# One strided four-column addition written as four one-column additions, in front of each scan of a recurrent layer

## The reference, cut to what matters

```python
dt = softplus(einsum('blhr,dr->blhd', dt_x, dt_proj_w) + dt_proj_b)
A = -exp(A_log)
def step(h, inp):
    dt_t, b_t, c_t, u_t = inp
    a_bar = exp(dt_t[..., None] * A[None, :, None, :])
    h = a_bar * h + (dt_t * u_t)[..., None] * b_t[:, :, None, :]
    y_t = einsum('bhds,bhs->bhd', h, c_t)
    return (h, y_t)
```

## Time and profile before

| | us |
|---|---|
| median of 3 runs | 17432.16 |
| the profiled execution | 17420.92 |
| its span (first to last instruction, slowest core) | 17419.6 |
| VectorE busy | 9252.5 (53%) |
| GpSimd busy | 6204.1 (36%) |
| TensorE matmuls busy | 5463.1 (31%) |
| ScalarE busy | 3186.6 (18%) |

### The profile page before, as it was taken

One profiled execution on the slowest core, in us unless ns is written; L12 is line 12 of the kernel. 1 busy time (PEld: TensorE's weight loads), 2 busy tenths in 40 slices (PEclk: granted clock), 3 DMA queues, 4 the chain that ended last, 5 costly groups with the idle time before them and its releaser, 6 DMA issues.

```text
span 17419.6 us, 75091 instructions; the slowest of 8 cores (17391.7 to 17419.6 us)
## 1 busy us (share of the span) xinstructions
PE 5463.1 (31%) x11019; PEld 1117.8 (6%) x11019; DVE 9252.5 (53%) x6045; ACT 3186.6 (18%) x3440; POOL 6204.1 (36%) x2692
## 2 busy tenths in 40 slices
PE   1123322222222222466553422222222222237555
PEld 0001000000000000011110100000000000001111
DVE  0023388888888888200003348888888888720011
ACT  0022322221222121100002331222122221101000
POOL 0000066666666666000000026666666666500000
DMA  2211100000000000210111110000000000020111
GB/s 54 64 41 35 49 4 4 4 4 4 4 4 4 4 4 3 62 35 23 42 44 41 36 44 4 4 4 4 4 3 4 4 4 4 15 72 16 31 41 41
DMA packets 760229, 378.17 MB, mean 22 GB/s; under 512 B 545528, under 2 KB 689112, under 8 KB 758752
## 3 DMA queue, kind: packets, MB, share of 16 engines
q1 hardware_dynamic: 759776, 373.37, 8.1%
HBM read 222.62 MB, written 148.91 MB: 21 GB/s over the span
## 4 chain that ended last, share of the span: by engine, by line
DVE 29%; DMA 21%; issue 16%; PE 16%; POOL 13%; ACT 3%; SPq 2%; DVEq 1%; POOLq 0%; ACTq 0%
DVE pf L269 19%; PE ps_mm L280 14%; POOL pb L234 13%; DVE pb L230 4%; DVE s_tmp L230 3%; ACT pf L275 2%; DMA s_rd<-g_dt 2%; DMA pb<-g_mid 2%; SPq L217 2%; PE ps_t L286 1%; DMA g_xsc<-colA 1%; DMA g_ct<-s_bc 1%; DMA g_bt<-s_bc 1%; DMA pf<-g_xn 1%; DVE pf L230 1%
## 5 line engine op out<-in xcount | busy, mean ns | idle before, releaser
L234 POOL TENSOR_TENSOR pb<-pb 128x2048 bf16<-128x2048 bf16 x768 | 3271.7, 4260 | 7720.2 <-ACT pb L275 5526.5
L269 DVE TENSOR_TENSOR_SCAN pf<-pf,pb 128x2048 f32<-128x2048 f32 x768 | 4090.4, 5326 | 607.5 <-DMA g_y<-s_yev 217.6
L234 POOL TENSOR_TENSOR pb<-pf,pb 128x512 bf16<-128x512 f32 x1920 | 2932.3, 1527 | 1243.9 <-DVE pf L269 951.1
L230 DVE TENSOR_TENSOR pb<-pf,pb 128x512 bf16<-128x512 f32 x1152 | 3024.5, 2652 | 141.5 <-DVE pf L269 135.2
L280 PE MATMUL ps_mm<-pb 128*128 128x512 bf16 x4608 | 2616.3, 589 | 1157.2 <-DMA pb<-g_y 288.2
L280 PE MATMUL ps_y<-pb,s_yd 128*16 128x512 bf16 x1536 | 799.8, 590 | 5145.3 <-DVE pb L230 4514.9
L275 ACT ACTIVATE pf<-ps_mm,s_acol 128x2048 f32<-128x2048 f32 x768 | 1441.5, 1977 | 2657.3 <-PE ps_mm L280 2657.3
L230 DVE TENSOR_TENSOR pf<-pf 128x512 f32<-128x512 f32 (+1 forms) x288 | 216.4, 751 | 1964.2 <-ACT pf L275 1045.2
L280 PE MATMUL ps_mm<-s_rd,s_pd 64*128 64x512 bf16 (+1 forms) x1024 | 596.4, 582 | 1723.7 <-ACT pf L275 1480.0
L225 DVE CAST pb<-pf 128x512 bf16<-128x512 f32 (+3 forms) x427 | 206.3, 494 | 1737.4 <-DMA pf<-g_xsc 599.1
L280 PE MATMUL ps_r<-pb,s_yd 128*16 128x512 bf16 x1536 | 830.9, 593 | 949.9 <-POOL pb L234 949.7
(11 more groups left out here) (70 smaller groups left out, 2544.0 us busy)
## 6 DMA issues: line engine op xcount, KB each, us to landing
pf<-x SPq DMA_DIRECT2D x64, 512.0 KB
g_xn<-pf SPq DMA_DIRECT2D x64, 256.0 KB
g_dt<-pb SPq DMA_DIRECT2D x256, 64.0 KB
s_rd<-g_dt SPq DMA_DIRECT2D x256, 64.0 KB
pf<-g_xn SPq DMA_DIRECT2D x64, 256.0 KB
g_x<-pf SPq DMA_DIRECT2D x64, 256.0 KB
g_mid<-pb SPq DMA_DIRECT2D x128, 128.0 KB
pb<-g_mid SPq DMA_DIRECT2D x128, 128.0 KB
```

Source lines behind the costliest of these rows:

```text
L230: o.tensor_tensor(out=d, in0=x, in1=y, op=op), waits)
L234: o.tensor_tensor(out=d, in0=x, in1=y, op=op), waits)
L269: return S.op("v", lambda o, d=dst, a0=d0, a1=d1: o.tensor_tensor_scan(out=d, data0=a0, data1=a1, initial=0.0, op0=ALU.mult, op1=ALU.add), ...
```

## The change

The addition of `s_tmp` to `w` at the 4 first positions is no longer one instruction on a pattern of 4 elements but a loop of 4 instructions, each on 1 element per partition. The first waits for `s_tmp` and for `w`; each later one waits for the one before it, and the memset for the last. What is computed is the same.

```diff
                 else:
                     m_t1 = vtt(s_tmp.ap(), a_seg, cs, ALU.mult,
                                waits=[m_exps[k][ti], m_carry[ti]])
-                    m_t2 = vtt(w_seg, w_seg, s_tmp.ap(), ALU.add,
-                               waits=[m_t1, m_w])
+                    m_t2 = m_t1
+                    for d in range(DH_SUB):
+                        wcol = AP(pb, w_i * 1024 + d * TC,
+                                  [[PB_N * 1024, 128], [1, 1]])
+                        m_t2 = vtt(wcol, wcol,
+                                   s_tmp.ap()[:, d:d + 1], ALU.add,
+                                   waits=[m_t2, m_w if d == 0 else None])
                     m_fx = vmemset(a_seg, 0.0, waits=[m_t2])
```

## The result

| | before | four columns |
|---|---|---|
| median of 8 runs, us | 17430.78 | 17930.91 |
| lowest to highest | 17416.53 to 17528.88 | 17923.64 to 17938.97 |
| ratio to before, 95% interval | | 1.0282 [1.0265, 1.0299] |
| span of the profiled execution | 17419.6 | 17929.1 |
| chunk with a carry, from scan to scan | 77.08 | 82.47 |

The change costs 500 us, 2.8%.

The account below looks back on a forecast made before the run. The prediction took one chain alternating between VectorE and GpSimd as the bound. Per chunk 1.18 + 3 x 0.95 + 2 x 1.32 = 6.67 us, over 96 chunks 640, gave 18,065 us, range 17,950 to 18,150.

Parts of the forecast that it names:

- One chain from scan to scan: Recurrences: work passes between VectorE and GpSimd, so instructions between `s_tmp` and scan lie on the path; 6.67 us per chunk.
- the rival that has GpSimd set the pace: Chunk head: columns fill VectorE's 7 to 8 us of idle time, giving 17,421 to 17,440 us; chance 0.02.
- The price of a step: Each extra column on VectorE: 0.315 us, 0.177 for the instruction and 0.14 for the wait behind it.
- the free tiles: Tiles 1, 3 and 5: GpSimd has finished its products, so three extra steps run unhindered, costing 0.95 us each tile.
- Columns 1 and 2 of tiles 2 and 4 held up: Tiles 2 and 4: the first two columns wait for GpSimd's products, costing 1.32 us per tile.
- The sum: Chunks with a carry: 6.67 us each over 96 chunks, 640 us in all.
- the won race: Rival, tiles 2 and 4: column 2 precedes GpSimd's third product, 1.01 us instead of 1.32; 18,002 us; chance 0.06.
- Tile 0: the second column waits for GpSimd's second `w`: Tile 0: column 1 gets in first, column 2 is held until that `w` ends, near 3.8 us; cost 1.18.
- Waits aren't free: Between dependent columns: 0.14 us per wait, against the skill's no-cost rule, with a step near 0.11, some 190 us.
- The errata figure: One-column addition: the skill's 58 cycles plus elements gives 61 ns, three free steps 0.61 us; set against 0.177 measured.
- The range: Whole kernel's time: from 17,950 us, past the rival with column 2 ahead, up to 18,150.

Follow-up runs that it names:

- vprod: The kernel before with all four products with C on VectorE, `w` still on GpSimd: 16817.46 us, ratio 0.9635.
- vall: The kernel before with `w` and all products with C on VectorE, GpSimd idle in the recurrence: 14554.02 us, ratio 0.8336.
- ms3: The kernel before with three chained memsets of a 128x4 scratch tile between its addition and its memset: 17671.14 us, ratio 1.0119.
- rep4: The kernel before with three more 128x4 additions (of zeros) behind its own, each waiting for the last: 17987.79 us, ratio 1.0299.
- late2: The four-column kernel with one more wait instruction, for something long done, ahead of column 2: 18033.01 us, ratio 1.0334 to the kernel before.
- late4: The four-column kernel with one more wait instruction, for something long done, ahead of column 4: 18027.90 us, ratio 1.0325 to the kernel before.
- nowait: The four-column kernel with no waits among the columns, only the first one waiting: 17642.31 us, ratio 1.0081 to the kernel before.

## Why the prediction was right or wrong, point by point

- **One chain from scan to scan, nothing of GpSimd left over to cover an extra instruction.** Right for tiles 1, 3 and 5, too strong for the others. VectorE's idle time at a chunk's head stayed at 711 us and the chunks without a carry at 70.1 us (70.0 with the change); nothing of the cost was hidden there, and the rival that has GpSimd set the pace, with a cost near nothing, is dead. vprod and vall show from the other side that the two engines take turns. But in tile 0 the scan waited 3.4 us for GpSimd and in tiles 2 and 4 0.6 us, and that time can be filled: ms3's three memsets cost 0.06 us or less there. The sum didn't suffer by it, since a column, other than a memset, waits for GpSimd itself. I had also misread the products: in tiles 0 to 3 they follow `w` after 0.20 us; GpSimd is idle only ahead of those of tiles 4 and 5.
- **The price of a step, 0.315 us. This is the step that failed.** The mechanism was right, an instruction and the wait behind it, one after the other; the size was not. A step is 0.267: 0.163 for the instruction and 0.104 for the wait. I had read the wait off the distance from the addition to the memset, 0.14, but what follows a column is another addition. The earlier trace rows had the right number: `s_tmp` ends at 4046.45 and the addition starts 0.17 later behind *two* waits. A second wait instruction adds 0.07 (the distance between the two in the trace), which leaves 0.10 for one, and in vall, where only one wait stands between them, 0.10 is what the rows show. rep4 confirms it for additions of 4 elements (0.28 apart), ms3 gives the memset's 0.20 (0.06 and 0.14). Three steps, and 0.01 off the last, shorter addition, make 0.79 for the 0.95 that I had; the free tiles paid 0.83, 0.77 and 0.74, tile 0 1.08 instead of 1.18.
- **Columns 1 and 2 of tiles 2 and 4 held up, 1.32 us.** Wrong, and mostly by the same error. The memset at 4058.83 came 0.03 behind GpSimd's product. An addition starts 0.04 sooner than a memset would, and the first column ends 0.01 sooner than the addition of 4 elements did, so column 2 comes 0.02 ahead. I gave this rival 0.06 and weighed it with the memset's start. These tiles paid 0.97 and 1.00. late2 against late4 shows the race itself; losing it costs a whole step more, 0.27 x 192 = 51 us.
- **The sum.** 96 x 5.39 = 517 us in the recurrences, against 640. The lost 123 us are some 50 of the race and some 70 of the step. Putting one of them right would not have been enough: the won race alone gives 18,002, since I had costed it with the long step, and the right step with the race lost about 17,990.
- **Tile 0: the second column waits for GpSimd's second `w`.** Right, 3.84 us in the rows.
- **Waits aren't free.** Right to set the rule aside: with it (the Trainium skill, VectorE: DVE Perf Modes, The DRAIN you can't avoid) the waits would cost nothing, and nowait shows that 390 of 517 us go with them. Without them an addition starts every 0.07 us. What that section of the Trainium skill measured are copies back to back; no run here has those.
- **The errata figure.** The 61 ns estimated for a column from the Trainium skill stand against 0.163 us measured. The later form in the same section of the Trainium skill (VectorE: DVE Perf Modes, The TRN2 errata), given for fp32 additions, (N + 151) cycles at 0.96 GHz for N elements, gives an estimate of 0.158, and the trace agrees with that one within 3%. What does come near 61 ns is the distance at which columns without a wait start in nowait, 0.07 us.
- **The range.** It reached down only as far as the won race, with 50 us to spare, though I had written that no row showed an addition of one column and had the memset's 0.06 as a lower bound. A step of 0.27 lay within that bound, and both errors pull the same way.

## What to carry to other kernels

A chain of short instructions costs more by its waits than by its work: 0.27 us a step here with a wait, 0.07 without. The wait depends on which instruction comes behind it, so read the gap between the same two kinds, and take off 0.07 us for each wait instruction beyond the first. Where an instruction of either engine holds up the other, a few hundredths of a microsecond decide who goes first, so a forecast should carry both outcomes. Time in which an instruction waits inside its recorded length is room for others that don't wait, as the memsets of ms3 show. And an engine that looks half idle beside a partner may be the one that makes the partner wait: add up what both hold the port for, and try the work on the faster one alone.

## What the runs showed of the hardware

- While GpSimd runs a tensor_tensor, VectorE instructions with two inputs wait for its end, even with one element per partition (0.16 us alone, 1.12 held up), and a memset doesn't (0.06 us). I had not expected how fine the order is cut: a lead of 0.02 us was enough (late4), in rep4 even one of 0.006 us (the median of tiles 2 and 4, where 181 of 192 second additions weren't held up); a lag of 0.03 us lost (the products at 4039.30 behind `w` at 4039.28, both rounded).
- A short instruction that gets in ahead hardly holds up GpSimd. Its third product takes 1.153 us in the kernel before, 1.157 when it starts 0.022 behind a column in the changed one, and 1.176 when it starts 0.006 behind an addition in rep4 (medians of tiles 2 and 4). By these numbers an estimate is that the addition keeps GpSimd out for 0.03 us of its own 0.16 to 0.18.
- The same `w` of 128x2048 in bf16 takes 1.23 us on VectorE and 4.05 on GpSimd. A product of 128x512 takes 0.68 on VectorE, where the next one starts after 0.60, and 1.15 to 1.36 on GpSimd. Since the two take turns, GpSimd's help cost this kernel 2.9 ms of 17.4.
- Two independent VectorE instructions overlap: columns without waits start every 0.07 us though each is recorded at 0.155.
- A scan of 128x512 takes 1.20 us and 0.06 more with an initial value from memory; one of 128x2048 takes 4.42.
